# Two transformer blocks on one core: the first attention's scores taken twice, in 32-row and 32-column tiles, with its batches interleaved

## The reference, cut to what matters

```python
h = rms_norm(x, norm1_w)
qkv = h @ w_qkv                                  # q, k, v: [B, 16, 256, 16]
q, k = rms_norm(q, q_scale), rms_norm(k, k_scale)
q, k = apply_rope(q, k, S, Dh)
gamma = sigmoid(silu(h @ gg_w1) @ gg_w2)         # one number per token
valid = (rel >= 0) & (rel < 64)
s = where(valid, einsum('bhqd,bhkd->bhqk', q, k) * scale, -inf)
w = softmax(s)
q_mem = einsum('bhqk,bhkd->bhqd', w * 0.9 ** rel * gamma[key], k)
attn_out = einsum('bhqk,bhkd->bhqd', w, v) @ w_o
mem_out = poly(silu(q_mem @ mem_w1)) @ mem_w2
x = x + attn_out * sigmoid(mem_out)
```

## Time and profile before

| | us |
|---|---|
| median of three runs | 799.58 (799.15 to 800.03) |
| the profiled execution | 799.59 |
| its span, first to last instruction | 797.8 |
| TensorE busy in it | 703.8 (88%) |
| VectorE, ScalarE, POOL busy | 469.2, 324.4, 248.0 |

### The profile page before, as it was taken

How to read it: one execution, slowest core, us unless ns; L and a number is a source line. 1 busy time by engine, 2 the same in 40 slices (tenths; PEclk the granted TensorE clock), 3 DMA queues, 4 the chain that set the end, 5 groups by cost and what they waited for, 6 DMA issues and landing times.

```text
span 797.8 us, 11864 instructions
## 1 busy us (share of the span) xinstructions
PE 703.8 (88%) x4468; PEld 580.5 (73%) x4468; DVE 469.2 (59%) x1058; ACT 324.4 (41%) x773; POOL 248.0 (31%) x330
## 2 busy tenths in 40 slices
PE   4986599999888699867799998988599999999997
PEld 2764378788777588756677776766488888888886
DVE  4789777776437686564565546473654444444444
ACT  2424144554533233323676674664232222222221
POOL 1236510100324722314434432343423334333400
PEclk9989699999999799979899998999799999999999
DMA  6323000000112100000100000001111111111001
GB/s 215 100 66 97 14 1 1 2 1 1 47 37 63 44 18 21 1 20 24 38 1 2 2 1 1 1 2 39 39 28 53 41 40 40 51 48 41 1 1 53
DMA packets 11672, 25.82 MB, mean 32 GB/s; under 512 B 1344, under 2 KB 3392, under 8 KB 11584
## 3 DMA queue, kind: packets, MB, share of 16 engines
q1 hardware_dynamic: 11616, 25.07, 10.9%
HBM read 24.02 MB, written 1.05 MB: 31 GB/s over the span
## 4 chain that ended last, share of the span: by engine, by line
PE 71%; DVE 17%; ACT 5%; issue 4%; POOL 1%; DMA 1%; SPq 0%; DVEq 0%; ACTq 0%; POOLq 0%
PE ps L555 45%; PE ps L650 4%; PE ps L621 4%; PE ps L838 3%; PE ps L633 3%; PE ps L826 3%; PE ps L816 2%; DVE NB L1172 1%; PE ps L563 1%; ACT AO L1107 1%; PE ps L691 1%; PE ps L624 1%; PE ps L577 1%; DVE sml L1513 1%; ACT PB L1095 1%
## 5 line engine op out<-in xcount | busy, mean ns | idle before, releaser
L1696 POOL TENSOR_SCALAR PB<-PB,sml 128x256 f32<-128x256 f32 x128 | 59.1, 483 | 96.9 <-DVE sml L1530 96.9
L1024 ACT CAST VVh<-U 128x512 fp32r<-128x512 f32 x50 | 31.0, 620 | 128.0 <-PE ps L555 99.9
L1368 DVE TENSOR_TENSOR U<-U,ps 128x512 f32<-128x512 f32 x50 | 34.3, 687 | 73.9 <-PE ps L555 73.9
L555 PE MATMUL ps<-ATh,wh 128*128 128x512 f32 x176 | 72.5, 412 | 5.4 <-POOL wl L1667 2.5
L555 PE MATMUL ps<-ATh,wl 128*128 128x512 f32 x176 | 71.2, 405 | 0.0
L555 PE MATMUL ps<-ATl,wh 128*128 128x512 f32 x176 | 71.1, 404 | 0.0
L1665 POOL TENSOR_SCALAR wh<-wr 128x768 fp32r<-128x768 f32 (+3 forms) x31 | 24.1, 777 | 140.6 <-PE ps L555 140.4
L1095 ACT ACTIVATE PB<-ps,sml 128x256 f32<-128x256 f32 x128 | 59.5, 492 | 12.7 <-DVE sml L1524 12.7
L1380 DVE TENSOR_TENSOR VVl<-U,VVh 128x512 fp32r<-128x512 f32 x50 | 40.5, 811 | 36.9 <-ACT VVh L1024 36.9
L650 PEld LDWEIGHTS ps<-VK,PT 128*128 128x128 f32 x384 | 49.3, 191 | 12.0 <-issue 11.4
L1667 POOL TENSOR_TENSOR wl<-wr,wh 128x768 fp32r<-128x768 f32 (+3 forms) x31 | 55.6, 1793 | 2.6
(11 more groups left out here) (257 smaller groups left out, 2051.7 us busy)
## 6 DMA issues: line engine op xcount, KB each, us to landing
wr<-in_w SPq DMA_DIRECT2D x32, 384.0 KB, 3.1
wr<-in_w SPq DMA_DIRECT2D x16, 321.0 KB, 3.0
wr<-in_w SPq DMA_DIRECT2D x11, 256.0 KB, 2.6
XO<-in_x SPq DMA_DIRECT2D x2, 512.0 KB, 4.7
out_dram<-XO SPq DMA_DIRECT2D x8, 128.0 KB, 1.7
wr<-in_w SPq DMA_DIRECT2D x2, 416.0 KB, 6.1
AO<-in_sm SPq DMA_DIRECT2D x1, 448.0 KB, 7.3
SELf<-in_sel SPq DMA_DIRECT2D x1, 352.0 KB, 3.9
```

Of the source, the lines that this page charges most:

```text
L555: t = x.matmul(o, a, b, start=first and i == 0 and c == 0, stop=last and i == n - 1 and c == 2, skip_group_check=skip)
L1368: x.tensor_tensor(b[:, :], a[:, :], bank("u", run, j, half)[:, :], ALU.mult).then_inc(*vacates("u", run, j, half))
L1696: t = x.tensor_scalar(p[:, c, :], p[:, c, :], m[:, 16 + c:17 + c], 1.0, ALU.mult, ALU.mult)
```

## The change

The plan: batches 0 and 1 are projected and rotated in the head stage, batches 2 and 3 inside the attention. Each batch goes through `score`, `turnmx`, `expo`, `weigh`, `weighed`, `parted`.

- q and k are rotated into QR with the cosine product before the scaling by 1/rms (`rope`), then summed on POOL and scaled on VectorE (`finish`), and every head is copied beside itself, so a head has 32 columns. `turnqk` turns 8 instead of 4 blocks a tile. After it, a head's 32 rows hold -high and low of q (QT), -high and high of k (KH) and k's low part (KL).
- `score`: two 32-row tiles at a time, into a pair of PSUM banks, one fp32r term, only for the maximum. VectorE keeps the maxima in MX; nothing is subtracted.
- `turnmx`: two transposes give the maxima by queries (MXT).
- `expo`: the scores again, keys by queries, as QT with KH, QT with KL, and a third matmul that subtracts the maximum. ScalarE takes the exponential of both banks at once; probabilities lie with the keys on the partitions, so `pturn` is gone.
- `weigh`: per four heads, four 32-column tiles, fp32: once with VK (v and scaled k alternating), once with ones for the sum in all rows.
- `weighed`: reciprocal on VectorE, product with 0.9 ** q on POOL, product on VectorE into XF.
- SP moves XF's even and odd partitions into XV and XM (64 partitions, 64 KB each), `parted` splits these into high (ScalarE) and low (POOL) parts of BT and AT. `turnqm` and `turnat` are gone; `oproj` 0 to 3 go behind the attention.

```diff
+    for u in range(6):
+        item("score", 0, u)
+    item("turnmx", 0)
+    for b in range(4):
+        later = 1 <= b < 3
+        item("expo", b, 0)
+        if b:
+            item("weighed", b - 1, 2)
+            item("weighed", b - 1, 3)
+            item("parted", b - 1, 1)
...
+        if later:
+            item("headnorm", b + 1)
+            item("rope", 2 * b + 2)
+            item("rope", 2 * b + 3)
+        item("expo", b, 1)
...
+        item("expo", b, 4)
+        item("weigh", b, 0)
+        item("expo", b, 5)
+        item("weigh", b, 1)
+        item("weighed", b, 0)
...
+        item("turnqk", 2 * b + 2)
+        item("weighed", b, 1)
+        item("turnqk", 2 * b + 3)
+        item("score", b + 1, 0)
+        item("weigh", b, 2)
+        item("score", b + 1, 1)
+        item("parted", b, 0)
+        item("score", b + 1, 2)
+        if b < 2:
+            item("project", 2 * b + 4)
...
+        item("turnmx", b + 1)
+        item("weigh", b, 3)
...
+        def score(b, u):
...
+            for i in range(2):
+                x.matmul(bk[:, i, 0:nf * w_], identb[:, :], (mb1 if qt else mb0)[:, :].unsqueeze(1).to_broadcast([128, nf, w_]),
+                         start=True, stop=False)
+            for k in range(nf):
+                f = fs.start + k
+                for i in range(2):
+                    r = slice(64 * sp + 32 * i, 64 * sp + 32 * i + 32)
+                    p = x.matmul(bk[:, i, k * w_:(k + 1) * w_], QT[r, f, qt * 128:qt * 128 + 128], KH[r, f, keys], start=False,
+                                 stop=k == nf - 1)
...
+        def expo(b, u):
...
+            for k in range(nf):
+                f = fs.start + k
+                for c in range(3):
+                    for i in range(2):
+                        r = slice(64 * sp + 32 * i, 64 * sp + 32 * i + 32)
+                        p = x.matmul(bk[:, i, k * w_:(k + 1) * w_], (KH[r, f, ks], KL[r, f, ks], SLT[r, f, :])[c],
+                                     MXT[b % 2][r, qs] if c == 2 else QT[r, f, qs], start=False, stop=k == nf - 1 and c == 2)
...
+        def weigh(b, f):
...
+            for what in range(2):
+                o = 256 if what else 0
+                for kt in range(2):
+                    q0, q1 = (128, 256) if kt else (0, 192)
+                    for c in range(4):
+                        u = (0 if kt else 2 + f // 2 * 2) + c // 2
+                        p = x.matmul(bk[32 * c:32 * c + 32, o + q0:o + q1], ON[:, :] if what else VK[:, 2 * b + kt, 4 * f + c, :, :].rearrange("p d s -> p (d s)"),
+                                     weights_of(b, u)[:, c % 2, f if kt else f % 2, :], start=kt == 0 and what == 0, stop=kt == 1,
+                                     skip_group_check=True)
...
+        def weighed(b, f):
...
+            x.reciprocal(RD[:, :], u[:, 256:512]).then_inc(*mark("rcp", k))
+            e.wait_ge(*at("rm", k))
...
+            x.tensor_tensor(XF[k % 2][:, :], u[:, 0:256], RM[:, :], ALU.mult).then_inc(*vacates("av", b, f))
...
+        def parted(b, g):
+            bs = slice(b * 256, b * 256 + 256)
+            for k in (4 * b + 2 * g, 4 * b + 2 * g + 1):
+                e.wait_ge(*at("moved", k))
+            e.wait_ge(*have("pv", 2 * b + 1))
+            x.copy(BT[0][:, g, bs], XV[:, :]).then_inc(*mark("hv", b, g))
+            x.copy(AT[0][:, g, bs], XM[:, :]).then_inc(*mark("hm", b, g))
...
+        def moved(b):
+            for f in range(4):
+                k, g = 4 * b + f, f // 2
+                r = slice(64 * (f % 2), 64 * (f % 2) + 64)
+                e.wait_ge(*vacated("av", b, f))
+                if k >= 2 and f % 2 == 0:
+                    e.wait_ge(*at("qm", (k - 2) // 4, (k - 2) // 2 % 2))
+                for to, first in ((XV, 0), (XM, 1)):
+                    x_.dma_start(to[r, :], XF[k % 2][first::2, :]).then_inc(*mark(f"moved{k % 2}", k, by=16))
...
         for name, _, _ in CHUNKS[NRAW:]:
+            if name == "mem4":
+                moved(0)
+                moved(1)
+            if name == "mem6":
+                moved(2)
+                moved(3)
```

More of the change, by code:

```diff
@@ L213, in plan @@
     item("tables")
-    item("fuse", 0)
-    item("fuse", 1)
-    item("turn1", 0)
[L217 to L236, removed]
-        if b == 3:
+    item("consts")
@@ new lines, in fuse @@
+    def fuse(*heads):
+        for h in heads:
+            item("fuse", h)
+    fuse(0, 1)
+    item("turn1", 0)
+    fuse(2)
+    item("project", 0)
+    fuse(3)
+    item("project", 1)
+    fuse(4, 5)
+    item("headnorm", 0)
+    item("rope", 0)
+    item("rope", 1)
+    fuse(6, 7)
+    item("finish", 0)
+    item("finish", 1)
+    fuse(8, 9)
+    item("turnqk", 0)
+    item("turnqk", 1)
+    fuse(10)
+    item("project", 2)
+    fuse(11)
+    item("project", 3)
+    fuse(12, 13)
+    item("headnorm", 1)
@@ L356, in plan @@
         item(*p[0])
-    return order, units, us
+    return order, us
 def build(nc, x, w, sm, sel, out):
@@ L424, in program @@
[L424 to L433, removed]
+    QKf = [sb(f"QKf{i}", [128, 512], ctx=l0) for i in range(2)]
@@ L469, in program @@
     m1.close()
-    order, units, us = plan()
+    order, us = plan()
     n_units = len(us)
@@ L480, in bank, with pair @@
         return banks[B.of(*key)]
+    def pair(*key):
+        return pairs[B.of(*key) - 8]
     def filled(*key):
@@ L654, in turnqm, with consts @@
-        def turnqm(half, k):
-            turn(ring["w"], ("tq", half, k), NB, half, k, lambda t: vacated("o", t // 2, 1, t % 2))
-        def turnat(half, k):
-            turn(ring["w"], ("ta", half, k), AO, half, k, lambda t: vacated("o", t // 2, 1, t % 2))
+        def consts():
+            e.wait_ge(*at("sm"))
+            b = fills(ring["w"], "dq")
+            for k in range(2):
+                t = x.matmul(b[:, k * 128:k * 128 + 128], small("dq")[:, k:k + 1].to_broadcast([128, 128]), ident, start=True,
+                             stop=True)
+            t.then_inc(*filled("dq"))
@@ L875, in spread @@
             p.then_inc(*filled("sp", half))
[L877 to L878 removed]
+        run(order, {"consts": consts, "fuse": fuse, "turn1": turn1, "project": project, "turnqk": turnqk, "l0begin": l0begin,
+                    "score": score, "turnmx": turnmx, "expo": expo, "weigh": weigh, "oproj": oproj,
                     "mlpbegin": mlpbegin, "step": step, "down": down, "memturn": memturn, "ffnturn": ffnturn, "up": up,
@@ L943, in turn1, with consts @@
                 turn(("t1", half, k), AT, half, k, small("nw")[:, k:k + 1])
+        def consts():
+            e.wait_ge(*have("dq"))
+            x.copy(DQ[:, :], bank("dq")[:, 0:256]).then_inc(*vacates("dq"))
+            e.wait_ge(*at("sm"))
+            x.copy(identb[:, :], ident)
+            e.wait_ge(*at("mask"))
+            x.copy(mb0[:, :], masks[:, 0:128])
+            x.copy(mb1[:, :], masks[:, 512:704]).then_inc(*mark("cb"))
         def project(t):
@@ new lines, in score @@
+        def score(b, u):
+            qt, sp, fs, keys = score_unit(u)
+            n = 512 if qt == 0 else 384
+            if b and u == 0:
+                e.wait_ge(*have("mt", b - 1))
+            e.wait_ge(*at("mxz"))
+            e.wait_ge(*have("s", b, u))
+            x.tensor_reduce(MX[:, qt, 2 * sp:2 * sp + 2, fs],
+                            pair("s", b, u)[:, :, 0:n].rearrange("p s (f k) -> p s f k", f=fs.stop - fs.start), AX_X,
+                            ALU.max).then_inc(*vacates("s", b, u))
```

504 lines of the change are left out of this document (259 added, 245 removed).

## The result

| | before | after |
|---|---|---|
| median (lowest to highest), us | 799.47 (799.15 to 800.03), 4 runs | 827.91 (825.97 to 828.07), 4 runs |
| span of the profiled execution, us | 797.8 | 826.3 |
| granted clock over the span | 0.948 | 0.905 |
| first matmul of the memory MLP, us | 203.16 | 228.02 |

The ratio is 1.0349, 95% interval 1.0331 to 1.0367: slower, where I had forecast 790 and faster, and outside my range. The head stage did what it should: the first score starts at 59.9 instead of 90.5. The attention then takes 168.1 us instead of 112.7, where the prediction named 140 as the sign that it would be wrong.

What follows compares the result with a forecast made beforehand. TensorE was taken to bound the attention, and to wait for rotated q and k before it. The attention ending 18 us earlier, less 5 and 3 at the memory MLP, gave 10 off 799.58: 790, range 765 to 808.

Steps and rivals of the forecast that it cites:

- Head stage: Before the attention: 10 us start, 43 of TensorE work, 4 of waits; first score at 57 instead of 90.5.
- TensorE's sum: TensorE's work in the attention: four batches of 23.3 us make 93, with work moved in from the head stage 109.
- rival 1: Attention: column tiles overlap fully (1.3 us a weighing group, not 2.1) and the reciprocal is cheap (0.42); 771 us, chance 0.20.
- The clock: Attention window expected at clock 1.00; one fall charged, 3.2 us, after a 5 us wait early in the memory MLP.
- Rival 3: Attention: the clock falls in the new waits, four more falls of 3.2 us, 13 in all; 803 us, chance 0.12.
- Waits: TensorE's waits inside the attention, following VectorE's order: some 19 us, making it 128 from its first score.
- the rotated tiles reach TensorE about when it is through with the exponentials: Attention, next batch's norm and rotation: this overlap hides nearly all of the 16.4 us waited for rotated q and k before.
- 7.5 us for unit 1's exponentials: Attention: unit 1's exponentials queue on ScalarE behind the previous batch's "parted"; 3 us late twice, 1.5 once.
- Reciprocal: VectorE's reciprocal of 128x256 in the attention's division: taken as 1.2 us, between 0.42 and 1.5 by two readings.
- Memory MLP: Its start: 5 us later relative to the attention's end, plus 3.2 for a fall of the clock after that wait.

Runs made afterwards that it cites:

- b2_scores32: The kernel before the change, with its 96 attention score matmuls contracting rows 0 to 31 only instead of all 128: 921.53 us.
- e6_rows64: e3_order with each pair of score matmuls on two 64-row tiles instead of two 32-row tiles, output then wrong: 797.88 us.
- e3_order: The changed kernel with parted(b-1,1) moved behind expo(b,3) and the next batch's two finish items behind expo(b,5), in every queue: 808.48 us.
- e5: e3_order with the reciprocal of the 128x256 sums replaced by a plain copy of the same size, weights left undivided: 801.79 us.

## Why the prediction was wrong

- **Head stage: right.** First score at 59.9 (predicted 57), with a wait of 2.7 for the banks of fuse (4) and 46.5 us of TensorE work (43).
- **TensorE's sum: too high at full clock.** The weighing group was 1.23, rival 1's price, not 2.1; 16 x 0.87 = 14 off 109 gives 95. The measured 129.60 us of busy time, with 34.86 at half clock and 94.74 at a mean of 0.78, is about 17.4 + 74 = 91 at full clock. A pair of score matmuls at 0.12 was right (0.21 at half clock), as were the reductions (0.956 and 1.218 for 0.95 and 1.22), the product (0.425) and the transfers (1.9 to 2.0 for 2.2).
- **The clock: the step that failed.** I summed all of the attention at 1.00. Measured: 0.72, and 0.50 through the first 36.6 us. It cost about 129.6 - 91 = 38 us. Rival 3 had the clock fall, and the first fall did come in a wait, of 2.73 us. What it lacked is that the clock does not come back afterwards: I took 3.2 us a fall and 13 in all. I had no row of a long stretch of sparse tiles. The 64-row pairs in the earlier trace rows are short and lie between full-array work, and I took their price without asking what the clock would do under many of them. b2_scores32 and e6_rows64 show that rows in use decide on it, not for how much of the 38 us.
- **Waits: 38.5 us (168.1 - 129.6) for my 19.** The step was "the rotated tiles reach TensorE about when it is through with the exponentials", together with 7.5 us for unit 1's exponentials. I listed finish's chain but did not ask what stands behind finish on ScalarE: the exponentials of units 2 and 3. That chain and "parted" made 22.6 us. e3_order takes this away and gains 19.4.
- **Reciprocal: 1.75 us for my 1.2**, above my bound of 1.5. The estimate of 2.3 worked out from the Trainium skill's repeat count of 8 (VectorE: DVE Perf Modes, "First, the fixed hardware budget") is as far off on the other side. By e5 the size was not decisive: all of the reciprocal's 21 us is worth 6.7.
- **Memory MLP.** From its first matmul to the end of the span it is 594.6 before, 598.3 after: 3.7 us later, where I had 5 and 3.2.
- **The sum**: 3 for the first score, -18 for TensorE's work, 38 for its clock and 19.5 for waits, 4.5 less for the MLP: 38, as measured (828 - 790). The agreement is one of bookkeeping, as all terms but the forecast's are read from the same profile. Full overlap of the tiles (rival 1) came true and was still not enough.

The clock and the waits are not independent: taking the waits away in e3_order also cut the half-clock time in the attention, from 94 to 72 us. How the 38 us of clock divide between the sparse rows and the waits is open; e6_rows64 puts 10.6 us on going from a quarter to half of the rows a matmul, with the values changed too, and with that change the clock is still only 0.84.

## What to carry to other kernels

In these runs a matmul tile that uses few rows was priced twice: in its own time, and in the clock of everything around it. Where the work was bound by TensorE at a granted clock of 1.00, look at what share of it becomes sparse before counting the gain, and read the clock of the window, not only the busy time. In a queue that runs in order, put what waits for a long chain behind what TensorE needs next; ask of each item what stands behind it, not only when it is itself ready.

## What had not been expected of the hardware

- TensorE was busy without a gap for over 230 us at a granted clock of 0.50, with a third of its time in matmuls that contract 32 rows.
- Four fp32 matmuls in 32-column tiles, and four fp32r matmuls in 32-row tiles, ran side by side: 16 weighing matmuls in 1.23 us, four score matmuls in 0.11 us, the time that two take.
- The reciprocal of 128x256 out of PSUM: 1.75 us, where a copy of the same shape takes 0.417.
- Full-array masks in bf16, doubled, raised the clock in the attention from 0.72 to only 0.78, and the filler of 12 full-array matmuls ahead of the first score put off the fall of the clock by some 7 us without preventing it.
